# Field-pair tower on one core: single-tile transposes in the first part, gathers paced anew, finer signals at the end

## The chip, the cores and the metric

The kernel runs on 1 core of one Trainium2 chip. The metric is the device time of one execution in microseconds. The kernel before was timed three times: 1156.47, 1158.18 and 1160.94 us, with a median of 1158.18 us. The profile comes from another execution of the same kernel, which took 1160.57 us; its recorded span is 1158.8 us.

## The reference, cut to what matters

2048 samples have 40 ids each. Each id picks a row of 64 floats from its own table. For each of the 780 pairs of fields (i, j) there is a 64x64 matrix W, and the pair's value is `(e_i W) . e_j`. The 780 values and 16 dense numbers go through two layers with bias and ReLU (512 and 256 wide) and a last product to one number.

```python
e = jnp.stack([tbl_0[ids[:, 0]], ..., tbl_39[ids[:, 39]]], axis=1)   # 2048 x 40 x 64
viW = jnp.einsum('bpd,pde->bpe', e[:, i_idx, :], W)                  # 780 pairs
z = jnp.einsum('bpe,bpe->bp', viW, e[:, j_idx, :])
h = jnp.concatenate([z, dense_ctx], axis=1)
h = jnp.maximum(h @ W_top1 + b_top1, 0.0)
h = jnp.maximum(h @ W_top2 + b_top2, 0.0)
y = h @ W_top3
```

Everything is float32.

## The kernel before, in words

**Chunks, tiles, steps.** The samples are worked on in 4 chunks of 512. Two fields make a tile, so there are tiles 0 to 19. A chunk is 196 numbered steps; a step multiplies embeddings with weights on TensorE into one of three PSUM buffers `u`, and VectorE multiplies the result with the other embedding (`multiply`, L952 and L921). "Column" steps (L1038) then go through a second small matmul that sums (L1052). "Row" steps (L1024), 72 a chunk, are summed by ScalarE (L838, 16 pieces each), or by one VectorE reduction (L962), or by six GpSimd additions (L755), as lists fix in advance. Steps are counted through the kernel: chunk 1 begins at step 196, chunk 2 at 392, chunk 3 at 588. A step is over for the others when VectorE has made its product; the semaphore `prod_ready` counts that.

**The two parts of chunk 0.** Only chunk 0 is cut in two parts of 256 samples (q = 0 and 1), steps 0 to 97 and 98 to 195, so that work can begin when half of the gathers are in. There a column step is two columns of 256 samples ("two" steps).

**Gathers.** GpSimd issues an indirect DMA for each field and 128 samples (L734): 4 for a tile in a part, 8 for a tile in a whole chunk, 640 in all. Tiles 0 to 3 land in `first_fields`, the others in a ring of 4 tiles, `gathered`, in which a gather waits until the tile four before it has been transposed. From the second part on each gather also waits until a given step is over (`issue_step`): its due time minus 14 steps, or a steady pace, whichever is earlier. The steady pace of the second part begins at step `FIRST_PART` with 2 steps a field; that of chunks 1, 2 and 3 is in `CHUNK_STEPS`. GpSimd's own row sums stand in the same queue.

**Transposes.** TensorE transposes the gathered tiles (L996) two at a time, and ScalarE copies the pair into `emb` (L799, and L797 for a swapped copy of tile 4). `make_transpose_steps` puts each pair at a step: in the first part 2 steps before its first use, later `LANDING` steps after its last gather was issued. Transposes are put out in their list's order, so that one due early waits behind the one ahead of it in the list.

**The layers on top** of chunk c run in the middle of chunk c+1, in four groups at the steps of `TOP_STEPS`: they stand with the first transposes that come at least `TOP_FIRST` steps after the chunk's start. A group of layer 1 is 12 matmuls of 128x512 (L1084) and two of half height (L1090); the one group of layer 2 is 8 (L1096); the last layer is 8 small ones (L1103). ScalarE copies out each group with bias and ReLU (`copy_top`, L853). Those of chunk 3 stand alone at the kernel's end.

**What sets the order.** `make_order` writes one list, `ORDER`; TensorE, VectorE and ScalarE each go through it and take their own entries. GpSimd goes through `POOL_ORDER`. Nothing is reordered when it runs, so an instruction that waits holds all behind it on its engine.

In the words below T4 is the transpose of tile 4, T(4,5) of both at once.

Of the kernel before, what the change touches and what calls it, by code (L numbers as in the profile page):

```python
# [49 lines left out]
EARLY = 9  # L50
EARLY_EVERY = 2
# [8 lines left out]
TOP_FIRST = 18  # L60
# [120 lines left out]
def make_first():  # L181
# [5 lines left out]
    for q in range(PARTS):  # L187
# [202 lines left out]

def make_needs():
# [53 lines left out]


TRANSPOSES = [(c, i, q) for c in range(CHUNKS) for q in parts(c) for i in range(TSTEPS)]
TURN_OF = {x: n for n, x in enumerate(TRANSPOSES)}


def make_transpose_steps():

    out = []
    for c, i, q in TRANSPOSES:
        need = c * N + NEEDS[c, q, i]
# [8 lines left out]
        out.append((at, c, i, q))  # L464
# [145 lines left out]
def pair_tower(nc, ids, tables, w_pairs, w_rows, dense, w1, b1, w2, b2, w3, y):  # L610
# [6 lines left out]
    with ctx:  # L617
# [55 lines left out]
        top_ready = sem("top_ready")  # L673
        top_copied = sem("top_copied")
# [28 lines left out]
        def _(pool):  # L703
# [6 lines left out]
            def gather(c, q, t, e, s):  # L710
# [3 lines left out]
                if first and t < FT:  # L714
# [3 lines left out]
                    if c >= 2:  # L718
                        pool.wait_ge(rows_transposed, TURN_OF[c - 2, t // 2, len(parts(c - 2)) - 1] + 1)
                elif first and RING_USE[c, q, t] >= GRING:  # L720

                    at, part, tile = RING_ORDER[RING_USE[c, q, t] - GRING]
                    pool.wait_ge(rows_transposed, TURN_OF[at, tile // 2, part] + 1)
# [41 lines left out]
        def _(act):  # L765
# [19 lines left out]
            def copy_emb(c, i, q, o):  # L785
                act.wait_ge(rows_transposed, TURN_OF[c, i, q] + 1)
# [4 lines left out]
                if i == HUB // 2:  # L791
# [3 lines left out]
                    for h in (0, 1):  # L795
                        to, of = slice((1 - h) * DIM, (2 - h) * DIM), slice(h * DIM, (h + 1) * DIM)
                        nc.scalar.activation(emb_swap[to, c % 2, at], u[of, BUFFER[o], HUB % 2, at], ACT.Copy)  # L797
                first = emb_at(c, 2 * i)
                nc.scalar.activation(emb[:, first:first + 2, at], u[:, BUFFER[o], :, at], ACT.Copy).then_inc(emb_ready, 1)  # L799
# [41 lines left out]
            def copy_top(c, group, o):  # L841
                layer, first = TOPS[group]
                acc = u[:, BUFFER[o], :, :]
                act.wait_ge(top_ready, c * TOP_GROUPS + group + 1)
# [352 lines left out]
```

## Time and profile before

| | |
|---|---|
| median of 3 runs | 1158.18 us (1156.47 to 1160.94) |
| the profiled execution | 1160.57 us, span 1158.8 us |
| TensorE matmul busy | 1105.2 us (95%) |
| VectorE busy | 947.9 us (82%) |
| ScalarE busy | 859.5 us (74%) |
| GpSimd busy | 744.8 us (64%) |
| DMA | 98.02 MB, mean 85 GB/s |

TensorE is busy almost throughout, but "busy" there includes waiting inside the pipeline of matmuls; VectorE is busy 9 tenths or more in most slices between 58 and 319 us and has its long rests where a group of the top layers fills TensorE. GpSimd's 0.95 us for a gather is followed by about 0.3 us between two, so it is fully taken at 76% busy. The rows further down are from the timeline (start in us, length in us, engine, line, operation, result<-inputs, count, and in brackets how long the engine stood idle before it and what ended that), from the list of waits, and from tables of stretches.

### The profile page before, as it was taken

Reading aid. Unit: us, or ns where it says so; the run is one execution under the profiler, and the core shown is the slowest. Engines: PE = TensorE matmul, PEld = TensorE weight load, DVE = VectorE, ACT = ScalarE, POOL = GpSimd, SP = SyncE. Lnnn points to the kernel's source line nnn. Section 1 sums busy time; section 2 is a strip of 40 time slices with the busy share of each in tenths; the row PEclk is TensorE's granted clock in tenths of the full one; section 3 lists DMA queues with packets and bytes.
Section 4 is the critical chain, followed back from the end, with each engine's and each line's share of the span. In section 5 each row is a group of like instructions: output and inputs, shape, how many; then the busy total and the mean of one; then the engine's idle time right before and its main releaser. Section 6 shows DMA issues by size and latency. Waiting matters only on the chain.

```text
span 1158.8 us, 52361 instructions
## 1 busy us (share of the span) xinstructions
PE 1105.2 (95%) x21232; PEld 506.7 (44%) x21232; DVE 947.9 (82%) x830; ACT 859.5 (74%) x6607; POOL 744.8 (64%) x898
## 2 busy tenths in 40 slices
PE   2699989999999999999999999999999999999998
PEld 1356757665643333333363333333354333333333
DVE  0699878999859689999976689999984968999960
ACT  0677857999958569999965457898982845799971
POOL 7776777777756555778777567788777756522310
PEclk9999999999999999999999999999999999999999
DMA  6344444444423332232322232222222323211000
GB/s 187 83 121 131 125 121 121 130 139 130 103 52 87 86 88 72 76 86 76 77 63 78 71 93 76 76 78 77 77 68 49 94 73 93 70 58 58 19 3 18
DMA packets 60594, 98.02 MB, mean 85 GB/s; under 512 B 17072, under 2 KB 17088, under 8 KB 60352
## 3 DMA queue, kind: packets, MB, share of 16 engines
q1 hardware_dynamic: 35568, 64.57, 18.1%
q0 software_dynamic: 20480, 21.01, 9.3%
q10 hardware_dynamic: 4304, 9.09, 2.4%
q8 instruction: 167, 2.74, 1.0%
q14 instruction: 75, 0.61, 0.2%
HBM read 94.60 MB, written 0.01 MB: 82 GB/s over the span
## 4 chain that ended last, share of the span: by engine, by line
PE 76%; ACT 9%; POOL 5%; issue 5%; DVE 4%; DMA 1%; DVEq 0%; POOLq 0%
PE u L1038 30%; PE u L1024 18%; PE zacc L1052 15%; ACT row_prod L838 8%; PE u L1084 7%; PE u L996 3%; POOL gathered L734 3%; DVE prod L952 2%; PE u L1096 2%; POOL first_fields L734 1%; DVE row_prod L921 1%; POOL row_prod_p L755 1%; DMA gathered<-tbl,index 1%; PE u L1090 1%; PE u L1070 0%
## 5 line engine op out<-in xcount | busy, mean ns | idle before, releaser
L838 ACT ACTIVATE row_prod<-row_prod 128x64 f32<-128x64 f32 x3248 | 776.5, 242 | 65.9 <-DVE row_prod L921 65.7
L952 DVE TENSOR_TENSOR prod<-u,emb 128x1024 f32<-128x1024 f32 x496 | 588.8, 1217 | 102.0 <-PE u L1038 100.4
L734 POOL DMA_INDIRECT gathered<-tbl,index x512 | 484.7, 947 | 221.9 <-issue 121.5
L838 ACT ACTIVATION_READ_ACCUMULATOR row_prod<-row_prod 128x1 f32 x3248 | 613.1, 189 | 0.0
L1038 PE MATMUL u<-emb,weights 64*32 64x512 f32 (+1 forms) x9760 | 523.1, 507 | 3.5 <-DVE prod L952 2.1
L1024 PE MATMUL u<-row_weights,emb 64*32 64x512 f32 (+5 forms) x5632 | 337.7, 522 | 7.1 <-ACT emb L799 2.3
L1038 PEld LDWEIGHTS u<-emb,weights 64*32 64x32 f32 x9760 | 200.9, 107 | 235.7 <-issue 114.4
L921 DVE TENSOR_TENSOR row_prod<-u,first_fields 128x1024 f32<-128x1024 f32 x203 | 246.9, 1216 | 62.1 <-PE u L1024 61.8
L1052 PE MATMUL zacc<-prod,band 64*32 64x512 f32 (+1 forms) x4960 | 277.1, 504 | 0.7 <-DVE prod L952 0.5
L755 POOL TENSOR_TENSOR row_prod_p<-row_prod_p 128x512 f32<-128x512 f32 (+4 forms) x210 | 128.8, 614 | 90.8 <-DVE row_prod_p L921 77.1
L1024 PEld LDWEIGHTS u<-row_weights,emb 64*32 64x32 f32 x5632 | 118.4, 109 | 147.4 <-issue 56.7
L1052 PEld LDWEIGHTS zacc<-prod,band 64*32 64x32 f32 x4960 | 106.4, 107 | 115.4 <-issue 104.0
L734 POOL DMA_INDIRECT first_fields<-tbl,index x128 | 121.4, 948 | 49.9 <-issue 26.5
L799 ACT ACTIVATE emb<-u 128x1024 f32<-128x1024 f32 (+1 forms) x50 | 42.4, 849 | 86.5 <-PE u L996 86.3
L1084 PE MATMUL u<-z,w12s 128*128 128x512 f32 x192 | 85.6, 603 | 0.0
L853 ACT ACTIVATE h<-u,b1s 128x512 f32<-128x512 f32 x16 | 10.1, 684 | 80.6 <-PE u L1090 80.6
L1084 PEld LDWEIGHTS u<-z,w12s 128*128 128x128 f32 x192 | 36.4, 193 | 44.1 <-issue 43.7
L921 DVE TENSOR_TENSOR row_prod_p<-u,first_fields 128x1024 f32<-128x1024 f32 x42 | 51.1, 1217 | 4.5 <-PE u L1024 4.4
L921 DVE TENSOR_TENSOR row_prod_v<-u,first_fields 128x1024 f32<-128x1024 f32 x43 | 52.3, 1217 | 2.8 <-PE u L1024 2.6
L962 DVE TENSOR_REDUCE row_sums<-row_prod_v 128x16 f32<-128x1024 f32 x43 | 51.0, 1209 | 0.0
L996 PE MATMUL u<-ident,gathered 128*128 128x128 f32 x256 | 38.4, 284 | 13.2 <-DMA gathered<-tbl,index 12.8
L996 PEld LDWEIGHTS u<-ident,gathered 128*128 128x128 f32 x256 | 27.4, 142 | 40.7 <-DMA gathered<-tbl,index 14.4
(29 smaller groups left out, 151.9 us busy)
## 6 DMA issues: line engine op xcount, KB each, us to landing
weights<-w_pairs SPq DMA_DIRECT2D x155, 256.0 KB
row_weights<-w_rows SPq DMA_DIRECT2D x90, 256.0 KB
gathered<-tbl,index POOLq DMA_INDIRECT x512
w12s<-w_top ACTq DMA_DIRECT2D x8, 832.0 KB
first_fields<-tbl,index POOLq DMA_INDIRECT x128
w12s<-w_top ACTq DMA_DIRECT2D x4, 512.0 KB
index<-ids SPq DMA_DIRECT2D x1, 280.0 KB, 11.8
row_sums<-dense ACTq DMA_DIRECT2D x4, 32.0 KB
```

The lines of the kernel that those rows point to most:

```text
L734: pool.indirect_dma_start(out=to, out_offset=None, in_=tables[2 * t + e], in_offset=bass.IndirectOffsetOnAxis(ap=index[:, col:col + 1].bit ...
L755: nc.gpsimd.tensor_tensor(to, x[:, :, 0:width], x[:, :, width:2 * width], ALU.add).then_inc(rows_reduced_p if last else halved, 1)
L799: nc.scalar.activation(emb[:, first:first + 2, at], u[:, BUFFER[o], :, at], ACT.Copy).then_inc(emb_ready, 1)
L838: last = nc.scalar.activation(x, x, ACT.Copy, accum_out=row_sums[:, c % 2, s, q:q + 1])
L921: nc.vector.tensor_tensor(result, products, x, ALU.mult).then_inc(prod_ready, 1)
L952: nc.vector.tensor_tensor(result, products, x, ALU.mult).then_inc(prod_ready, 1)
L962: nc.vector.tensor_reduce(row_sums[:, c % 2, s, q:q + 2 * FF], x, mybir.AxisListType.X, ALU.add).then_inc(rows_reduced_v, 1)
L996: last = nc.tensor.transpose(u[:, b, h, s * P:(s + 1) * P], x, ident[:, :])
L1024: last = nc.tensor.matmul(u[g * TILE:(g + 1) * TILE, b, h, places], emb[half, emb_at(c, at // 2), samples_of], row_weights[half, x % PIECE ...
L1038: last = nc.tensor.matmul(u[of, b, h, to], weights[half, x % WRING, unit, of], y, start=True, stop=True)
L1052: last = nc.tensor.matmul(zacc[TILE * cg:TILE * cg + TILE, bank, samples(c, q)], band[half, TILE - 1 - r:2 * TILE - 1 - r], prod[half, (c ...
L1084: nc.tensor.matmul(u[:, b, m, :], w12s[:, x % 2, m * FULL + q, :], z_blocks(c, q)[:, 0, :], start=(q == 0), stop=False)
```

## The change

Five edits. In the first part of chunk 0 tiles 4 to 9 are transposed and copied one at a time, and `make_first` mixes the steps by single tiles, so that a row step of tile 4 may stand ahead of T5. `FIRST_PART` goes from 40 to 44 and `LANDING` of chunk 0 from 9 to 11, which puts the gathers of the second part 4 steps and its transposes 6 steps later. The pace of chunks 2 and 3 begins 3 steps earlier, and their transposes go with it, apart from T(10,11) of chunk 3 (step 609 in both). `TOP_FIRST` goes from 18 to 20; with the new steps that moves chunk 1's four top groups from steps 413, 433, 453, 473 to 430, 450, 470, 489; those of chunk 2 go from 609, 633, 653, 673 to 609, 630, 650, 670. And at the top ScalarE signals each copy by itself, a new semaphore `top_half` tells of the first half of a group, the half-height matmuls of layer 1's second group stand first in it, and layer 2's eight stand so that the first four need only layer 1's first two copies.

```diff
+SINGLE = range(4, 10)
-TOP_FIRST = 18
+TOP_FIRST = 20
-LANDING = (9, 17, 18, 18)
-FIRST_PART = 40
+LANDING = (11, 17, 18, 18)
+FIRST_PART = 44
-CHUNK_STEPS = {1: (115, 3.9), 2: (280, 4.9), 3: (480, 4.9)}
+CHUNK_STEPS = {1: (115, 3.9), 2: (277, 4.9), 3: (477, 4.9)}
...
-            for i in range(EARLY // 2 + 1):
-                now = [x for x in rows if max(tiles_used(x)) // 2 <= i]
-                ready = [x for x in twos if max(tiles_used(x)) // 2 <= i]
+            for t in [*range(1, SINGLE[0], 2), *SINGLE]:
+                now = [x for x in rows if max(tiles_used(x)) <= t]
+                ready = [x for x in twos if max(tiles_used(x)) <= t]
...
+def tiles_at(c, t, q):
+    return range(t, t + (1 if (c, q) == (0, 0) and t in SINGLE else 2))
...
-            def copy_emb(c, i, q, o):
-                act.wait_ge(rows_transposed, TURN_OF[c, i, q] + 1)
+            def copy_emb(c, t, q, o):
+                act.wait_ge(rows_transposed, TURN_OF[c, t, q] + 1)
...
-                first = emb_at(c, 2 * i)
-                nc.scalar.activation(emb[:, first:first + 2, at], u[:, BUFFER[o], :, at], ACT.Copy).then_inc(emb_ready, 1)
+                first, count = emb_at(c, t), len(tiles_at(c, t, q))
+                nc.scalar.activation(emb[:, first:first + count, at], u[:, BUFFER[o], 0:count, at], ACT.Copy
+                                     ).then_inc(emb_ready, 1)
...
                     for m in (0, 1):
+                        if m == 0 and group:
+                            act.wait_ge(top_half, c * (TOP_GROUPS - 2) + group)
+                        else:
+                            act.wait_ge(top_ready, c * TOP_GROUPS + group + 1)
                         to, bias = (h1, b1s) if layer == 1 else (h2, b2s)
-                        ins = nc.scalar.activation(to[:, first + m, :], acc[:, m, :], ACT.Relu,
-                                                   bias=bias[:, first + m:first + m + 1])
+                        nc.scalar.activation(to[:, first + m, :], acc[:, m, :], ACT.Relu,
+                                             bias=bias[:, first + m:first + m + 1]).then_inc(top_copied, 1)
...
-                    pe.wait_ge(top_copied, c * TOP_GROUPS + group)
-                    for m, q in itertools.product((0, 1), range(M1)):
+                    for m, q in ((0, 0), (1, 0), (0, 1), (1, 1), (1, 2), (0, 2), (0, 3), (1, 3)):
+                        if (m, q) == (0, 0):
+                            pe.wait_ge(top_copied, c * TOP_COPIES + LAYER1_COPIES[1])
+                        elif (m, q) == (1, 2):
+                            pe.wait_ge(top_copied, c * TOP_COPIES + LAYER1_COPIES[2])
+                        elif (m, q) == (0, 3):
+                            pe.wait_ge(top_copied, c * TOP_COPIES + LAYER1_COPIES[3])
...
-                    for q, g in itertools.product(range(M2), range(SUB)):
-                        last = nc.tensor.matmul(u[g * TILE:(g + 1) * TILE, b, 0, 0:P], w3s[:, q, :],
+                    for q in range(M2):
+                        pe.wait_ge(top_copied, c * TOP_COPIES + M1 + q + 1)
+                        for g in range(SUB):
+                            last = nc.tensor.matmul(u[g * TILE:(g + 1) * TILE, b, 0, 0:P], w3s[:, q, :],
```

TensorE's queue at the start, before: the transposes (`ident`) and the row steps of tiles 0, 4 and 5 to 7 (`row_weights`) behind steps 0 and 1.

```order
L996 MATMUL u<-ident,gathered 128x128 x4
...
L1024 MATMUL u<-row_weights,emb 32x128 x4
L1024 MATMUL u<-row_weights,emb 32x512 x16
L996 MATMUL u<-ident,gathered 128x128 x4
L1024 MATMUL u<-row_weights,emb 32x512 x24
L1038 MATMUL u<-emb,weights 32x256 x16
```

The same place now.

```order
L1025 MATMUL u<-ident,gathered 128x128 x2
...
L1053 MATMUL u<-row_weights,emb 32x128 x4
L1025 MATMUL u<-ident,gathered 128x128 x2
L1053 MATMUL u<-row_weights,emb 32x512 x16
L1025 MATMUL u<-ident,gathered 128x128 x2
L1053 MATMUL u<-row_weights,emb 32x512 x16
L1025 MATMUL u<-ident,gathered 128x128 x2
L1053 MATMUL u<-row_weights,emb 32x512 x16
L1067 MATMUL u<-emb,weights 32x256 x16
```

Before, T(4,5) stands ahead of steps 2 to 5 and T(6,7) ahead of steps 6 and 7. Now T4, T5, T6 and T7 stand apart, with two row steps (16 matmuls of 512) between them.

TensorE's queue at step 75, where the first transposes of the second part come, before.

```order
L1052 MATMUL zacc<-prod,band 32x256 x16
L996 MATMUL u<-ident,gathered 128x128 x4
L996 MATMUL u<-ident,first_fields 128x128 x8
L996 MATMUL u<-ident,gathered 128x128 x4
L1038 MATMUL u<-emb,weights 32x256 x16
L1024 MATMUL u<-row_weights,emb 32x512 x8
L1052 MATMUL zacc<-prod,band 32x256 x16
L1038 MATMUL u<-emb,weights 32x256 x48
L1052 MATMUL zacc<-prod,band 32x256 x16
L996 MATMUL u<-ident,gathered 128x128 x4
```

The same place now.

```order
L1081 MATMUL zacc<-prod,band 32x256 x16
L1025 MATMUL u<-ident,gathered 128x128 x4
L1025 MATMUL u<-ident,first_fields 128x128 x8
L1067 MATMUL u<-emb,weights 32x256 x16
L1053 MATMUL u<-row_weights,emb 32x512 x8
L1081 MATMUL zacc<-prod,band 32x256 x16
L1067 MATMUL u<-emb,weights 32x256 x16
L1025 MATMUL u<-ident,gathered 128x128 x4
L1067 MATMUL u<-emb,weights 32x256 x32
```

Four pairs stood together at step 75 (tiles 18 and 19 of the first part, tiles 0 to 5 of the second) and T(6,7) of the second part five steps behind. Now three stand together, T(4,5) comes at step 78 and T(6,7) at step 86.

TensorE's last queue entries, with the semaphores that they wait for, before.

```order
L1084 MATMUL u<-z,w12s 128x512 [waits w12_loaded0,z_copied]
L1084 MATMUL u<-z,w12s 128x512 x11
L1090 MATMUL u<-z,w12s 128x512 x2
L1096 MATMUL u<-h,w12s 128x512 [waits top_copied,w12_loaded1,z_copied]
L1096 MATMUL u<-h,w12s 128x512 x7
L1103 MATMUL u<-z,w3s 32x128 [waits top_copied,small_loaded]
L1103 MATMUL u<-z,w3s 32x128 x7
```

The same place now.

```order
L1111 MATMUL u<-z,w12s 128x512 [waits w12_loaded0,z_copied]
L1111 MATMUL u<-z,w12s 128x512
L1123 MATMUL u<-z,w12s 128x512 x12
L1140 MATMUL u<-h,w12s 128x512 [waits top_copied,w12_loaded1,z_copied]
L1140 MATMUL u<-h,w12s 128x512 x3
L1140 MATMUL u<-h,w12s 128x512 [waits top_copied]
L1140 MATMUL u<-h,w12s 128x512
L1140 MATMUL u<-h,w12s 128x512 [waits top_copied]
L1140 MATMUL u<-h,w12s 128x512
L1150 MATMUL u<-z,w3s 32x128 [waits top_copied,small_loaded]
L1150 MATMUL u<-z,w3s 32x128 x3
L1150 MATMUL u<-z,w3s 32x128 [waits top_copied]
```

The half-height pair has moved to the front of its group, and one wait for all copies has become several waits for one copy each.

## Rows read from the trace of the kernel before

**Rows 1.** Waits of TensorE: us in total, times, longest.
```profile
PE u L996 <- DMA first_fields<-tbl,index: 22.3, 4, 12.8
PE u L996 <- DMA gathered<-tbl,index: 12.8, 6, 3.4
```

**Rows 2.** Timeline of TensorE, steps 0 to 8: start, length, engine, operation, count, idle before.
```profile
25.80 5.07 PE L1024 MATMUL u<-row_weights,emb 64*32 64x256 f32 x112 [0.78 <-ACT emb L799]
...
34.86 5.84 PE L1024 MATMUL u<-row_weights,emb 64*32 64x320 f32 x112
...
44.27 0.44 PE L996 MATMUL u<-ident,gathered 128*128 128x128 f32 x2 [3.21 <-DMA gathered<-tbl,index]
44.63 4.50 PE L1024 MATMUL u<-row_weights,emb 64*32 64x512 f32 x48
```

**Rows 3.** Timeline of GpSimd: tile 7's last gather, three ring waits, chunk 1's tile 11.
```profile
41.84 0.95 POOL L734 DMA_INDIRECT gathered<-tbl,index  x1 [0.30 <-issue]
...
83.60 0.95 POOL L734 DMA_INDIRECT gathered<-tbl,index  x1 [0.79 <-PE u L996]
96.50 0.94 POOL L734 DMA_INDIRECT gathered<-tbl,index  x1 [3.20 <-PE u L996]
...
137.99 0.95 POOL L734 DMA_INDIRECT gathered<-tbl,index  x1 [1.76 <-PE u L996]
...
326.94 0.95 POOL L734 DMA_INDIRECT gathered<-tbl,index  x1 [0.31 <-DVE prod L952]
```

**Rows 4.** Timeline of VectorE: steps 8, 15, 75, 80, 83.
```profile
50.18 1.22 DVE L921 TENSOR_TENSOR row_prod<-u,first_fields 128x1024 f32<-128x1024 f32 x1
...
61.70 1.21 DVE L921 TENSOR_TENSOR row_prod<-u,first_fields 128x1024 f32<-128x1024 f32 x1
...
140.62 1.23 DVE L952 TENSOR_TENSOR prod<-u,emb 128x1024 f32<-128x1024 f32 x1 [2.47 <-PE u L1038]
...
150.82 1.23 DVE L921 TENSOR_TENSOR row_prod<-u,first_fields 128x1024 f32<-128x1024 f32 x1 [3.06 <-PE u L1024]
...
156.14 1.23 DVE L952 TENSOR_TENSOR prod<-u,emb 128x1024 f32<-128x1024 f32 x1 [0.53 <-PE u L1038]
```

**Rows 5.** ScalarE's groups by shape, 0 to 300 us: busy us, mean ns, idle before.
```profile
L799 ACT ACTIVATE emb<-u 128x512 f32<-128x512 f32 x20 | 11.8, 594 | 46.2 <-PE u L996 46.1
...
L797 ACT ACTIVATE emb_swap<-u 64x256 f32<-64x256 f32 x4 | 1.5, 379 | 9.4 <-PE u L996 9.3
```

**Rows 6.** Timeline of TensorE: T7 of the second part; T(10,11) of chunk 1.
```profile
149.26 0.44 PE L996 MATMUL u<-ident,gathered 128*128 128x128 f32 x2 [3.37 <-DMA gathered<-tbl,index]
...
336.51 1.09 PE L996 MATMUL u<-ident,gathered 128*128 128x128 f32 x8
```

**Rows 7.** Table of stretches: busy us and count per engine, granted clock, DMA.
```profile
152.00:154.00 2.00, 2.00 (x48) 1.24 (x40) 1.27 (x2) 1.92 (x16) 1.65 (x2) 0.50 0.67 161
```

**Rows 8.** Timeline of GpSimd: a row sum, and the first gather of chunk 3.
```profile
706.91 3.39 POOL L755 TENSOR_TENSOR row_prod_p<-row_prod_p 128x512 f32<-128x512 f32 x5
...
721.81 0.95 POOL L734 DMA_INDIRECT first_fields<-tbl,index  x1 [1.02 <-DVE prod L952]
```

**Rows 9.** Timeline of TensorE: T11 of chunk 3, top groups of chunks 2 and 3.
```profile
883.13 0.66 PE L996 MATMUL u<-ident,gathered 128*128 128x128 f32 x4 [2.32 <-DMA gathered<-tbl,index]
883.62 12.16 PE L1084 MATMUL u<-z,w12s 128*128 128x512 f32 x24
...
1134.10 10.57 PE L1084 MATMUL u<-z,w12s 128*128 128x512 f32 x24
```

**Rows 10.** The chain that ended last, in order of time: start, us, what.
```profile
1145.77 1.27 ACT h L853 x2
...
1147.18 7.12 PE u L1096 x16
...
1154.32 1.27 ACT z L853 x2
...
1155.73 0.68 PE u L1103 x16
```

More of the change, by code:

```diff
@@ L388 @@
 W12_BLOCKS = 2 * FULL + 1
+TOP_COPIES = M1 + M2 + 1
+LAYER1_COPIES = range(1, M1 + 1)
 def make_needs():
@@ L443, in issue_step, with make_transposes @@
     return max(1, int(min(in_time, steady)))
-TRANSPOSES = [(c, i, q) for c in range(CHUNKS) for q in parts(c) for i in range(TSTEPS)]
-TURN_OF = {x: n for n, x in enumerate(TRANSPOSES)}
+def tiles_at(c, t, q):
+    return range(t, t + (1 if (c, q) == (0, 0) and t in SINGLE else 2))
+def make_transposes():
+    out = []
+    for c in range(CHUNKS):
+        for q in parts(c):
+            t = 0
+            while t < T:
+                out.append((c, t, q))
+                t += len(tiles_at(c, t, q))
+    return out
+TRANSPOSES = make_transposes()
+TURN_OF = {(c, x, q): n for n, (c, t, q) in enumerate(TRANSPOSES) for x in tiles_at(c, t, q)}
 def make_transpose_steps():
     out = []
-    for c, i, q in TRANSPOSES:
-        need = c * N + NEEDS[c, q, i]
+    for c, t, q in TRANSPOSES:
+        i = t // 2
+        need = c * N + min(n for n, s in enumerate(STEPS[c]) if part_of(c, n) == q and {*tiles_at(c, t, q)} & {*tiles_used(s)})
         if c == 0 and q == 0:
@@ L463, in make_transpose_steps @@
             assert issued <= at <= need
-        out.append((at, c, i, q))
+        out.append((at, c, t, q))
     return out
@@ L673, in pair_tower @@
         top_ready = sem("top_ready")
+        top_half = sem("top_half")
         top_copied = sem("top_copied")
@@ L718, in gather @@
                     if c >= 2:
[L719 removed]
+                        pool.wait_ge(rows_transposed, TURN_OF[c - 2, t, len(parts(c - 2)) - 1] + 1)
                 elif first and RING_USE[c, q, t] >= GRING:
                     at, part, tile = RING_ORDER[RING_USE[c, q, t] - GRING]
[L723 removed]
+                    pool.wait_ge(rows_transposed, TURN_OF[at, tile, part] + 1)
                 if issue_step(c, q, 2 * t + e, s):
@@ L983, in buffer_free, with transpose_step @@
                 else:
-                    pe.wait_ge(top_copied, last[1] * TOP_GROUPS + last[2] + 1)
-            def transpose_step(c, i, q, b):
-                for h in (0, 1):
-                    t = 2 * i + h
+                    pe.wait_ge(top_copied, last[1] * TOP_COPIES + min(2 * last[2] + 2, TOP_COPIES))
+            def transpose_step(c, first, q, b):
+                for h, t in enumerate(tiles_at(c, first, q)):
                     if t < FT:
@@ L1014, in pair_step @@
                 t = max(tiles_used(step))
-                if (c, q, "tile", t // 2) not in seen:
-                    seen.add((c, q, "tile", t // 2))
-                    pe.wait_ge(emb_ready, TURN_OF[c, t // 2, q] + 1)
+                if (c, q, "tile", t) not in seen:
+                    seen.add((c, q, "tile", t))
+                    pe.wait_ge(emb_ready, TURN_OF[c, t, q] + 1)
                 if step[0] == "row":
@@ L1078, in top_group, with remainder @@
                 if layer == 1:
+                    def remainder(start):
+                        for m in (0, 1):
+                            half = slice(m * DIM, (m + 1) * DIM)
+                            last = nc.tensor.matmul(u[:, b, m, :], w12s[half, x % 2, 2 * FULL, :], z_blocks(c, FULL)[half, 0, :],
+                                                    start=start, stop=not start)
+                        return last
+                    if first:
+                        remainder(True)
                     for m in (0, 1):
@@ L1083, in top_group @@
                                                             (c, q // 2, len(parts(c)) - 1)])
-                            nc.tensor.matmul(u[:, b, m, :], w12s[:, x % 2, m * FULL + q, :], z_blocks(c, q)[:, 0, :],
-                                             start=(q == 0), stop=False)
+                            last = nc.tensor.matmul(u[:, b, m, :], w12s[:, x % 2, m * FULL + q, :], z_blocks(c, q)[:, 0, :],
+                                                    start=(first == 0 and q == 0), stop=(first > 0 and q == FULL - 1))
@@ L1086, in top_group @@
+                        if first and m == 0:
+                            last.then_inc(top_half, 1)
                     if first == 0:
                         pe.wait_ge(z_copied, Z_COPY[c, ROW_BLOCK + 2, 0])
-                    for m in (0, 1):
-                        half = slice(m * DIM, (m + 1) * DIM)
-                        last = nc.tensor.matmul(u[:, b, m, :], w12s[half, x % 2, 2 * FULL, :], z_blocks(c, FULL)[half, 0, :],
-                                                start=False, stop=True)
+                        last = remainder(False)
```

19 lines of the change are left out of this document (10 added, 9 removed).

## The prediction

> **What bounds the kernel now.** I read the waits of TensorE first: its named waits are mostly for gathers, 22.3 us for tiles 0 to 3 and 12.8 us for later tiles in six waits [rows 1]. The first sum is not touched by the change. Then I read the start in the timelines. GpSimd issues a gather every 1.25 us (0.95 us and 0.30 us between), so a tile of the first part needs 5.0 us of issue; tile 7's last one ends at 42.79 and its transpose starts at 44.27, 1.5 us later [rows 2, 3]. TensorE stood idle 3.21 us for it, with steps 6 and 7 queued behind although they need only tile 5. VectorE catches up from step 8 on: between its start at 50.18 and step 15 at 61.70 stand ten operations, 1.15 us apart, with no idle time beyond 0.1 us between two [rows 4]. From there into the 130s it is VectorE that sets the pace, so what is gained before step 8 is kept until something else comes last.
>
> Two later places stand out. At 149.26 the transpose of tile 7 of the second part waits 3.37 us for its gather, and after it the granted clock is 0.50 (1.2 GHz) for a while [rows 6, 7]. At 883.13 T11 of chunk 3 waits 2.32 us, and the 24 matmul records of the top group behind it take 12.16 us where the same group takes 10.57 us at the kernel's end, at full clock [rows 9]. At the end TensorE waits twice for two ScalarE copies of 1.27 us together [rows 10].
>
> **Term A, the start.** Before, steps 2 to 5 stand behind T(4,5), which waits for tile 5, and end at 40.70 (34.86 + 5.84) [rows 2]. Now T4 needs tile 4 alone, whose last gather ends 15.0 us before tile 7's, at 27.8, so that it lands at 29.3, before step 1 ends at 30.87. T4 takes about 0.4 us (44.27 to 44.63 for the two matmuls of T7), so steps 2 and 3 start at 31.3; T5 (landed 34.3) and steps 4 and 5 follow and end at 37.5 at the latest if the steps keep their 5.84 us. Tile 6 lands at 39.3. T6 and steps 6 and 7 need 0.4 us and at most 2 x 1.5 us (44.63 + 4.50 is three such steps at the slower rate [rows 2]), so TensorE is through at 42.7, before tile 7 lands at 44.3. T7 ends at 44.7, step 8 takes 0.9 to 1.5 us, and VectorE starts step 8 at 45.6 to 46.2 instead of 50.18: the same ten operations follow, since the five reductions on VectorE keep their places among them. That is 4.0 to 4.6 us; I take 4.4. Tiles 8 and 9 land 5 and 10 us after tile 7, at 49.3 and 54.3, before VectorE's queue asks for them (steps 15 and 19); T(10,11) at step 21 then meets tile 11, landing at 64.3, at about 63, which costs TensorE up to 1.4 us, within its buffers' lead.
>
> ScalarE gets six copies of 128x256 for three of 128x512. A copy of 512 takes 594 ns, one of 256 elements 379 ns on 64 partitions [rows 5]; so two cost 0.16 us more than one, 0.5 us in all. Between two copies it sums rows and has gaps: 46.2 us of its idle time stands ahead of such copies [rows 5]. I cost them at 0, bounds 0 and 0.5 us. The Trainium skill, "Perfetto Trace Analysis", Optimizing Scalar/DVE Operations, speaks against this edit: each ScalarE instruction carries a fixed access cost (some 50 ns of busy time on PSUM), so larger ones are better where the engine is saturated. By its figure the three extra copies would cost an estimated 0.15 us, by the rows 0.5 us; the page also says that breaking up helps where the engine isn't saturated but makes others wait, which is the case here.
>
> **Term B, the seam between the parts.** Before, four pairs of transposes stand together at step 75 and VectorE idles 2.47 us; T(6,7) at step 80 waits 3.37 us and then half clock follows, and VectorE's idle time from step 75 to step 83 adds to 7.34 us (2.47, 0.17, 3.06, 0.43, 0.68, 0.53) [rows 4]. Now T(6,7) stands at step 86. Without waits step 86 comes some 6 x 1.15 = 7 us behind step 80, and the wait was 3.4 us: it is gone if the lead of 4.4 us is matched by GpSimd. It is: GpSimd's stream is without idle time apart from three waits for the ring, 0.79, 3.20 and 1.76 us, less the usual 0.30 each: 4.85 us [rows 3]. These wait for T(12,13), T(14,15) and T(18,19), which all come as much earlier as the steps do. What stays is three pairs together (2.47 x 3/4 = 1.9 us) and two single ones at 0.5 us each (0.53 in rows 4 as the nearest). Gain 7.3 - 2.9 = 4.4 us; bounds 2 and 5.
>
> The pace of 44 and the transposes 6 steps later (which free the ring later) could hold GpSimd: of the second part tile 16's first gather now needs step 107 over and T(12,13) at step 110, tile 18's needs step 115 over and T(14,15) at step 118. With steps 8.8 us earlier than before and gathers 4.4 us earlier these fall within about 1 us of each other. I take no delay, bound 2 us.
>
> **Does the lead of 8.8 us survive chunk 1?** GpSimd issues without a break until tile 11 of chunk 1, whose last gather ends at 327.89 and lands at 329.4; its transpose stands at 336.51, 7.1 us later [rows 3, 6]. TensorE gains 8.8 us, GpSimd 4.4: 2.7 us of room are left. From tile 12 on gathers wait for steps and move along.
>
> **Term C, chunk 3.** GpSimd's stream is again full from the first gather of chunk 3 at 721.81, which waited for step 479 to end [rows 8], to tile 11. It now needs only step 476, about 3.4 us earlier, but a row sum of 3.6 us (3.39 and a last 0.22) for step 475 stands ahead of it now: it starts at about 719.0. Behind it, up to tile 11, stand 96 gathers as before and 10 row sums instead of 11. Tile 11 lands 2.8 + 3.6 = 6.4 us earlier in relation to the steps, T(10,11) stays at step 609, and the wait of 2.32 us goes with the slow stretch behind it (12.16 - 10.57 = 1.6 us): 3.9 us. The other transposes of chunks 2 and 3 come 3 steps earlier like their gathers. Chunk 1's top groups move 17 steps later; their own work is the same, I cost the move at 0, bounds -2 and +2 us, the size of one wait with its slow stretch.
>
> **Term D, the end.** Layer 2's first four matmuls need only copies that were made 10 us before, so the gap between 1145.77 and 1147.18 goes, 1.4 us. Its copies: h2's first half is copied beside the last matmul, so only one of two remains: 0.6 us. Half of the sixteen records of L1103 (0.68 us [rows 10]) run beside the second copy: 0.3 us. Together 2.3 us, bounds 1.4 and 2.7. The same edits in chunks 0 to 2 are hidden: TensorE has steps behind each group.
>
> **Sum.** 4.4 + 4.4 + 3.9 + 2.3 = 15.0 us. Against the profiled execution: 1160.57 - 15.0 = 1145.6. That execution is 2.4 us above the median of 1158.18, so the median after is 1143.2; I say 1143. By the bounds: the most is 4.6 + 5 + 4 + 2.7 + 2 = 18 us (1140), the least 4.0 + 2 + 3.9 + 1.4 - 2 - 0.5 = 9 us (1149).
>
> **The rivals.**
> 1. *The lead is given back to the gathers in chunk 1 (15%).* For it: the room of 2.7 us is small, and the later pace and ring waits can hold GpSimd in the second part. If GpSimd gains nothing, TensorE can be ahead by 7.1 us at 336.51, not 8.8, and the wait may bring one more slow stretch of 1.6 us: 1143 + 1.7 + 1.6 = 1146. If it comes 3 us later than before, 1149. Against it: each of the three ring waits shrinks with the steps.
> 2. *The start brings no lead (8%).* Idle time moves: TensorE now idles from 37.5 to 39.3 and before T7, and the clock may be at 1.2 GHz then. If steps up to 8 go at the slow rate and VectorE starts step 8 no earlier, term A is 0: 1147. The Trainium skill, "TensorE: Matmul & The Clock Gate", What's actually happening, says that the slow clock is the default and activity lifts it, so that rests between short bursts are what it punishes; of the half clock behind a rest rows 7 show an instance. Against it: tile 7's landing, not TensorE's rate, sets step 8.
> 3. *Chunk 3's wait stays (9%).* The top groups of chunk 1, now nearer to chunk 3's gathers, hold back GpSimd, and tile 11 is late as before: term C is 0, 1147.
> 4. *Slower than before (4%).* The same mechanism, larger: gathers wait while a top group fills TensorE, about 10 us for a layer-1 group (10.57 in rows 9). If two groups more fall into the issue of chunk 2's last tiles, chunk 3's stream starts some 17 us late. Its transposes at steps 532 to 609 have about 7 to 8 us of room (as the 7.1 us in chunk 1), so TensorE waits 9 us and after each of five waits a slow stretch follows, 8 us: 17 us lost against 11 won without term C, and 1164. It decides from about 12 us of delay on. Against it: groups at 430 to 489 are all but one over before the stream's first gathers are due at step 477.
> 5. *Only the end is faster (4%).* The edits of the first part cancel each other, 1155 to 1158.
>
> **Chances and range.** The forecast has 60%. Measurement tells about 0.5%, 5.8 us, from no change. Faster by more than that (below 1152.4) are the forecast, rivals 1 to 3: 0.90 with small losses to the neighbours; same 0.06, slower 0.04. The range of 8 in 10 holds the forecast with its bounds and rivals 1 to 3: 1137 to 1152.
>
> **What would show it.** In the profile after: steps 2 to 7 ahead of T7, VectorE's step 8 near 46; no wait of TensorE near 145 and no stretch at half clock there; T(10,11) of chunk 1 without a wait near 328; no wait for a gather at step 609 and 10.5 us for the group behind it; layer 2 right behind layer 1 at the end. Wrong would be a wait for gathers between 225 and 330, a step 8 later than 48, or the last 35 us shorter by less than 1.4 us.

## The result, and the profile after

The changed kernel takes 1145.96 us (median of 5, 1144.97 to 1146.48) beside 1158.12 us before (median of 5, 1156.15 to 1160.94): ratio 0.9893, 95% interval 0.988 to 0.9906. The forecast was 1143, range 1137 to 1152. The profiled execution took 1146.02 us (span 1144.2), against 1160.57 (span 1158.8) for the one before: 14.6 us less where the sum said 15.0.

The waits of TensorE after (us in total, times, longest), which answer to [rows 1]:

```profile
PE u L1025 <- DMA first_fields<-tbl,index: 22.1, 4, 13.1
PE u L1025 <- DMA gathered<-tbl,index: 3.0, 1, 3.0
PE u L1053 <- ACT emb L824: 3.0, 3, 1.3
PE u L1053 <- ACT z L843: 2.1, 1, 2.1
...
PE u L1150 <- ACT z L883: 0.3, 1, 0.3
```

Of six waits for later tiles (12.8 us) one of 3.0 us is left. The first tiles' 22 us are the same, as nothing touches them.

TensorE's timeline at the start after, for [rows 2] (start, length, engine, line, count, idle before):

```profile
31.27 4.17 PE L1053 MATMUL u<-row_weights,emb 64*32 64x320 f32 x80
35.37 0.44 PE L1025 MATMUL u<-ident,gathered 128*128 128x128 f32 x2
35.74 2.13 PE L1053 MATMUL u<-row_weights,emb 64*32 64x512 f32 x32
40.91 0.41 PE L1025 MATMUL u<-ident,gathered 128*128 128x128 f32 x2 [3.04 <-DMA gathered<-tbl,index]
41.25 3.63 PE L1053 MATMUL u<-row_weights,emb 64*32 64x512 f32 x32
44.81 0.44 PE L1025 MATMUL u<-ident,gathered 128*128 128x128 f32 x2
```

The wait now stands at T6, and the two steps behind it take 3.63 us where the two behind T5 take 2.13: it is followed by half clock (granted clock 0.50 from 41.4 to 44.6).

VectorE after, for [rows 4]: the products of steps 6, 8 and 15, then steps 75, 80 and 86 at the seam.

```profile
43.29 1.22 DVE L951 TENSOR_TENSOR row_prod<-u,first_fields 128x1024 f32<-128x1024 f32 x1 [2.68 <-PE u L1053]
...
46.89 1.22 DVE L951 TENSOR_TENSOR row_prod<-u,first_fields 128x1024 f32<-128x1024 f32 x1
...
58.78 1.23 DVE L951 TENSOR_TENSOR row_prod<-u,first_fields 128x1024 f32<-128x1024 f32 x1 [0.24 <-PE u L1053]
...
136.91 1.22 DVE L982 TENSOR_TENSOR prod<-u,emb 128x1024 f32<-128x1024 f32 x1 [1.84 <-PE u L1067]
...
144.52 1.21 DVE L951 TENSOR_TENSOR row_prod<-u,first_fields 128x1024 f32<-128x1024 f32 x1
...
151.73 1.22 DVE L982 TENSOR_TENSOR prod<-u,emb 128x1024 f32<-128x1024 f32 x1 [0.34 <-PE u L1067]
```

Against before that is 3.3 us earlier at step 8, 2.9 at step 15, 3.7 at step 75, 6.3 at step 80 and 7.8 at step 86, which starts at 159.5 before. I compared the start of the same step's product in both traces further on as well:

| step | before | after | difference |
|---|---|---|---|
| 8 | 50.2 | 46.9 | -3.3 |
| 75 | 140.6 | 136.9 | -3.7 |
| 86 | 159.5 | 151.7 | -7.8 |
| 140 | 231.2 | 224.0 | -7.2 |
| 300 | 468.0 | 461.0 | -7.0 |
| 355 | 533.0 | 527.8 | -5.3 |
| 588 | 850.8 | 842.9 | -7.9 |
| 609 | 898.1 | 886.0 | -12.0 |
| 783 | 1119.0 | 1107.2 | -11.8 |
| end of span | 1158.8 | 1144.2 | -14.6 |

So the time went in four places: the start, the seam, step 609 and the end. Later places in TensorE's timeline after, for [rows 6] and [rows 9]: T(6,7) of the second part, T(10,11) of chunk 1, a new wait near step 354, and T(10,11) of chunk 3 with the top group behind it.

```profile
149.94 0.66 PE L1025 MATMUL u<-ident,gathered 128*128 128x128 f32 x4
...
329.34 1.09 PE L1025 MATMUL u<-ident,gathered 128*128 128x128 f32 x8
...
525.44 1.09 PE L1053 MATMUL u<-row_weights,emb 64*32 64x512 f32 x16 [1.25 <-ACT emb L824]
...
872.45 1.09 PE L1025 MATMUL u<-ident,gathered 128*128 128x128 f32 x8
873.38 10.46 PE L1123 MATMUL u<-z,w12s 128*128 128x512 f32 x24
```

The waits of 3.37 and 2.32 us are gone, and the group of 24 takes 10.46 us instead of 12.16. There is no half clock behind T(6,7) either; the table of stretches has, for 150 to 152 us (us; busy us and count of PE, PEld, DVE, ACT, POOL; granted clock; DMA share; GB/s):

```profile
150.00:152.00 2.00, 2.00 (x53) 1.14 (x60) 1.66 (x3) 1.37 (x9) 1.60 (x2) 1.00 0.16 39
```

GpSimd's gather for tile 11 of chunk 1 stands here:

```profile
323.30 0.94 POOL L758 DMA_INDIRECT gathered<-tbl,index  x1 [0.30 <-issue]
```

It ends 3.6 us earlier than before (324.24 for 327.89), lands at about 325.7 if 1.5 us pass as behind tile 7 in [rows 3], and is wanted at 329.34: 3.6 us of room, where 2.7 were forecast.

The chain that ended last, from the last group on, for [rows 10]:

```profile
1123.25 10.50 PE u L1123 x24
1133.75 6.88 PE u L1140 x16
1140.63 0.02 issue
1140.65 0.69 ACT z L883
1141.35 0.04 issue
1141.39 0.47 PE u L1150 x8
1141.86 0.02 issue
1141.88 0.28 ACT h L887
```

Layer 2 follows layer 1 without a copy between them, one copy of 0.69 us stands where two took 1.27, and 8 records of layer 3 are left on the chain instead of 16. From the last product (step 783) to the end of the span it is 37.0 us for 39.8.

### The profile page after: what moved, and what is told of

Its sections match the earlier page's. It is cut to its first block, busy times and chain, and to the rows that moved or that the text cites. A ratio compares the mean times of both kernels' runs of the same rounds, so it can differ in the third digit from the quotient of the medians.

```text
span 1144.2 us, 52390 instructions
## 1 busy us (share of the span) xinstructions
PE 1103.2 (96%) x21232; PEld 507.6 (44%) x21232; DVE 947.9 (83%) x830; ACT 860.4 (75%) x6610; POOL 742.7 (65%) x898
## 4 chain that ended last, share of the span: by engine, by line
PE 81%; ACT 8%; DVE 4%; issue 3%; POOL 2%; DMA 1%; DVEq 0%
PE u L1067 32%; PE u L1053 19%; PE zacc L1081 16%; ACT row_prod L864 7%; PE u L1123 7%; PE u L1025 3%; DVE prod L982 3%; PE u L1140 2%; POOL first_fields L758 1%; DVE row_prod L951 1%; POOL gathered L758 1%; PE u L1111 1%; DVE row_sums L992 1%; PE u L1099 0%; ACT emb L824 0%
## 5 line engine op out<-in xcount | busy, mean ns | idle before, releaser
L1067 PEld LDWEIGHTS u<-emb,weights 64*32 64x32 f32 x9760 | 203.2, 107 | 233.9 <-issue 111.0
L824 ACT ACTIVATE emb<-u 128x1024 f32<-128x1024 f32 (+2 forms) x53 | 42.8, 810 | 85.5 <-PE u L1025 81.8
L1025 PEld LDWEIGHTS u<-ident,gathered 128*128 128x128 f32 x256 | 27.3, 141 | 31.9 <-issue 12.8
## 6 DMA issues: line engine op xcount, KB each, us to landing
index<-ids SPq DMA_DIRECT2D x1, 280.0 KB, 11.8
```

The costliest lines, as they stand in the source:

```text
L824: nc.scalar.activation(emb[:, first:first + count, at], u[:, BUFFER[o], 0:count, at], ACT.Copy).then_inc(emb_ready, 1)
L1025: last = nc.tensor.transpose(u[:, b, h, s * P:(s + 1) * P], x, ident[:, :])
L1067: last = nc.tensor.matmul(u[of, b, h, to], weights[half, x % WRING, unit, of], y, start=True, stop=True)
```

## The experiments

The theory was that the gain is the sum of four independent parts: the end (2.3 us), the single tiles (4.4), the pace with the seam (4.4) and chunk 3 (3.9). Its rivals were that the single tiles and the pace only work together, that chunk 3's wait goes by itself once the front is earlier, and that the end's edits are hidden. All kernels are the changed one with some of its edits undone. The one with the end alone is this:

```diff
-SINGLE = range(4, 10)
+SINGLE = ()
-TOP_FIRST = 20
+TOP_FIRST = 18
-LANDING = (11, 17, 18, 18)
+LANDING = (9, 17, 18, 18)
-FIRST_PART = 44
+FIRST_PART = 40
-CHUNK_STEPS = {1: (115, 3.9), 2: (277, 4.9), 3: (477, 4.9)}
+CHUNK_STEPS = {1: (115, 3.9), 2: (280, 4.9), 3: (480, 4.9)}
...
-            for t in [*range(1, SINGLE[0], 2), *SINGLE]:
+            for t in range(1, 10, 2):
```

**Four parts, first series.** The end alone, as above:

> Only the end's edits (copies signalled one by one, the half-height matmuls first, layer 2 reordered); steps, gathers and transposes as before. Theory: it acts at the kernel's end alone, since in chunks 0 to 2 TensorE has steps behind every group. The trace of the changed kernel ends 37.0 us after the start of the last VectorE product, that of before 39.8 us: 2.8 us, so 1158.1 - 2.8 = 1155.3 us. The waits of 3.4 us near 149 us and 2.3 us near 883 us stay. Rival: the finer signals also free ScalarE or PSUM buffers in the middle; then it is faster by over 4 us, below 1154.

The end and single tiles (`SINGLE` and its loop as in the changed kernel):

> The end's edits and the single transposes of tiles 4 to 9 with their step order; FIRST_PART, LANDING, CHUNK_STEPS and TOP_FIRST as before. Theory: the lead of the start (2.9 us from step 15 to step 60 in the changed kernel's trace) is carried through, since GpSimd's three ring waits shrink with it; the wait for tile 7 of the second part near 149 us and its half clock stay: 1155.3 - 2.9 = 1152.4 us. Rival: the lead is lost at the seam, where TensorE only waits longer for the gathers (4 to 6 us instead of 3.4): 1155.

The end and the pace (`FIRST_PART = 44`, `LANDING = (11, ...)`):

> The end's edits and FIRST_PART 44 with LANDING 11; pairs of transposes at the start and the old step order. Theory: the transpose of tiles 6 and 7 of the second part at step 86 no longer waits, and the slow stretch behind it goes; the changed kernel's lead grew from 3.0 to 8.3 us there and kept 7.2 us from step 140 on, so 4.3 us are kept: 1155.3 - 4.3 = 1151 us. Rival: this needs the start's lead too, because without it GpSimd is held by the pace of 44 (tile 16 waits for step 107 instead of 103), runs late into chunk 1, and TensorE waits for gathers between 225 and 330 us: 1154 or slower.

The end, single tiles and the pace:

> The end's edits, the single transposes and FIRST_PART 44 with LANDING 11; CHUNK_STEPS and TOP_FIRST as before. Theory: the gains add, 2.8 + 7.2 = 10.0 us by the traces, 1148.1 us, and the wait near 883 us (now near 876) stays. What is missing to the changed kernel's 1146.0 is then the worth of the edits to chunks 2 and 3, about 4 us by the traces' lead at step 610 (12.0 against 7.7 us), which would give 1150. Rival: the wait in chunk 3 is no longer there although its pace is unchanged, and the kernel stands at 1146.

These ran on a chip where the kernel before takes 1651.05 us instead of 1158. There they gave, as ratios to it: e1 0.9985 [0.9969, 1.0002], e2 0.9932 [0.9905, 0.9958], e3 0.9975 [0.9956, 0.9994], e4 0.9912 [0.9884, 0.9939]. None of the microseconds expected can be read off such a chip. Among these four the single tiles give most, and the pace adds nothing clear of the noise by itself (the intervals of e1 and e3 overlap). That this order holds at 1158 us is not shown; the traces there give the seam more than the start.

**Chunk 3 with the end** (`TOP_FIRST = 20`, `CHUNK_STEPS` 277 and 477):

> The end's edits, CHUNK_STEPS 277 and 477 and TOP_FIRST 20; the first part, FIRST_PART and LANDING as before. The four runs before this one ran at 1641 to 1651 us, the kernel before too (1651), with TensorE waiting for its own instructions; if this run is at 1158 us again for the kernel before, then: theory, the wait of 2.3 us for tile 11 of chunk 3 and the slow stretch behind it go, 4.3 us, and the end gives 2.8 us: 1158.1 - 7.1 = 1151 us, with the wait near 149 us still there. Rival: without the lead of the first chunk nothing changes for chunk 3's gathers relative to the steps, so the sum is the same; but if moving chunk 1's top groups by 17 steps costs something that the changed kernel's trace hides, it stands at 1153 or above.

0.9932 [0.9907, 0.9956], again on the 1651 us chip. There the gain beyond the end is some 9 us by the ratios, as much as that of the single tiles and twice what was expected; why, I didn't settle. That TensorE waits for its own instructions on this chip, as the expectation has it, no run shows: its profile has gaps with no wait named.

**The end alone, again.** The same kernel as e1:

> The kernel of e1 (only the end's edits) once more, to see whether the kernel before is at 1158 or at 1651 us this time. Theory: at 1158 it gives 2.8 us at the end and nothing elsewhere, 1155.3 us. If the kernel before is at 1651 us again, then about 2.4 us as in e1 (1648.7 against 1651.1), since the end's edits take away waits for ScalarE that TensorE's slower issue does not hide. Rival: the finer signals also help in the middle, over 4 us.

This ran on a chip of the first kind: 1156.83 us beside 1159.22, ratio 0.9976 [0.9965, 0.9987], so 2.8 us by the ratio and 2.4 by the medians. The end's edits are not hidden. TensorE's timeline of it, T7 of the second part and T11 of chunk 3:

```profile
151.13 0.69 PE L1025 MATMUL u<-ident,gathered 128*128 128x128 f32 x2 [3.11 <-DMA gathered<-tbl,index]
...
883.68 0.66 PE L1025 MATMUL u<-ident,gathered 128*128 128x128 f32 x4 [2.36 <-DMA gathered<-tbl,index]
884.18 12.16 PE L1123 MATMUL u<-z,w12s 128*128 128x512 f32 x24
```

Both waits and the slow group are there as in [rows 6] and [rows 9]: nothing is gained in front of the end, whose last product starts 0.6 us later than before (1119.63 and 1118.98).

**Second series of parts.** The same kernels as e2 to e5, the end with single tiles, with the pace, with both, and with chunk 3:

> The kernel of e2 (end's edits and the single transposes with their step order, all else as before), where the kernel before runs at about 1158 us. Theory: the lead of 2.9 us is carried through, because GpSimd's ring waits shrink with the steps; the wait near 149 us (now near 146) stays at about 3 us with its half clock. 1158.5 - 2.4 (measured for the end alone) - 2.9 = 1153 us. Rival: the lead is lost at the seam, the wait there grows to 5 or 6 us, and the kernel is at 1156.

> The kernel of e3 (end's edits and FIRST_PART 44 with LANDING 11), same setting. Theory: no wait for tile 7 of the second part and no half clock after it; the seam gives 5.3 us at step 86, of which about 1 us is given back by step 140: 1156.1 - 4.3 = 1152 us. Rival: without the start's lead the pace of 44 holds GpSimd back and TensorE waits for gathers in chunk 1 (225 to 330 us), with another stretch at half clock: 1155 or slower.

> The kernel of e4 (end, single transposes, FIRST_PART 44, LANDING 11; chunks 2 and 3 as before). Theory: the gains add: 1156.1 - 2.9 - 4.3 = 1149 us, and the wait for tile 11 of chunk 3 stays and makes up the remaining 3 to 4 us to the changed kernel. Rival: that wait is gone by itself and the kernel is within 1 us of 1146.

> The kernel of e5 (end's edits, CHUNK_STEPS 277 and 477, TOP_FIRST 20; first part as before). Theory: the wait near 883 us and the half clock behind it go, 4 us, nothing else: 1156.1 - 4 = 1152 us. Rival: the moved top groups and transposes of chunk 2 cost or give something of their own, over 1.5 us either way (in the changed kernel's trace the lead went from 7.0 us at step 300 to 5.3 at step 355 and to 7.5 at step 535).

They ran on another chip where the kernel before takes 1650.92 us, and repeat the first series within its intervals: 0.9942 [0.9918, 0.9965], 0.9972 [0.9954, 0.999], 0.9913 [0.9887, 0.9938] and 0.9941 [0.9919, 0.9964].

**The end, single tiles and pace, once more** (the kernel of e4 and e9):

> The kernel of e4 and e9 (end, single transposes, FIRST_PART 44 and LANDING 11; chunks 2 and 3 as before), once more, for a chip on which the kernel before runs at about 1158 us. Theory: the end is worth 2.4 us (measured), start and seam together 7.2 us by the traces' lead at step 300, the wait for tile 11 of chunk 3 stays: 1158.5 - 9.6 = 1149 us. Rival: the wait of chunk 3 is gone by itself, 1146; or start and seam are worth only what is left of 12.2 when 2.4 and 4.3 are taken off, 5.5 us, 1150.5. If the kernel before is at 1651 us again, 1637 as in e4 and e9.

1149.44 us beside 1159.43, ratio 0.9912 [0.9897, 0.9928]. From e6's 0.9976 that is 7.4 us for single tiles and pace together. The rest to the changed kernel's 0.9893 is 2.2 us for chunk 3 by the ratios, 3.5 us by the medians (1149.44 to 1145.96, on two occasions on which the kernel before differs by 1.3 us). The intervals of these two ratios overlap (0.9897 to 0.9928, 0.988 to 0.9906), so the worth of chunk 3's edits by themselves rests on the traces. Its timeline at T11 of chunk 3:

```profile
876.75 0.66 PE L1025 MATMUL u<-ident,gathered 128*128 128x128 f32 x4 [2.39 <-DMA gathered<-tbl,index]
877.24 10.47 PE L1123 MATMUL u<-z,w12s 128*128 128x512 f32 x24
```

That refutes the rival: the steps in front of it come 6.4 us earlier than before, and the wait is still 2.39 us. Chunk 3's stream of gathers begins when a step is over, so it came earlier with the steps (first gather at 715.66 instead of 721.81) and nothing was won against them. It takes the edits to `CHUNK_STEPS` and `TOP_FIRST` to remove the wait; which of the two does it, no run separates. But the group behind it takes 10.47 us, not 12.16. Its table of stretches (us; busy us and count of PE, PEld, DVE, ACT, POOL; granted clock; DMA share; GB/s):

```profile
880.00:884.00 4.00, 4.00 (x10) 1.72 (x10) 0.00 (x0) 0.00 (x0) 3.29 (x5) 1.00 0.13 25
```

The same place in the kernel before:

```profile
884.00:888.00 4.00, 4.00 (x7) 1.62 (x6) 0.00 (x0) 0.85 (x1) 2.96 (x4) 0.57 0.14 25
```

The clock stayed at 2.4 GHz (1.00) here, and was down for most of the stretch (0.57) there, after waits of the same length (2.39 and 2.32 us).

**A version beyond the change.** In the changed kernel TensorE waits 2.08 us at 314.01 for ScalarE's copy of z, since row sums of a later chunk stand in ScalarE's queue ahead of it. The edit holds them back past the turn:

```diff
-            if held or j < len(order) and steps < HOLD and order[j][0] != "turn":
+            if held or j < len(order) and steps < HOLD and (order[j][0] != "turn" or order[j][1] < o[1]):
...
-            out += held
-            held = []
+            out += [x for x in held if x[1] <= o[1]]
+            held = [x for x in held if x[1] > o[1]]
...
-        if o[0] in ("transpose", "top", "copy z") and (i + 1 == len(order) or order[i + 1][0] != "top"):
+        if (o[0] in ("transpose", "top", "copy z") or o[0] == "turn" and o[2]) and (i + 1 == len(order) or order[i + 1][0] != "top"):
```

> The changed kernel with one more edit: ScalarE's row sum of step 202 (which belongs to chunk 1) no longer stands ahead of the copy of chunk 0's first turned rows but behind that copy and the one of T(8,9); the sum of step 210 goes behind the second turned copy. The computation is the same. [...] The copy of the turned rows starts when it is ready, about 309 us, and not at 312.96 us, so the wait of 2.1 us at 314 us goes, and with it the half clock at 314.4 us (3.4 us long, 1.7 us of work lost): 3.8 us, 1146.0 - 3.8 = 1142 us (ratio to the kernel before 0.986). Rival: the wait goes, but TensorE and VectorE meet the next wait at once, since ScalarE is fully busy there and step 210 needs the ring place that the sum of step 202 frees later now: 1145 to 1146, ratio 0.989. If it is a chip on which the kernel before runs at 1651 us, nothing follows.

1144.26 us (median of 4, 1142.9 to 1145.97) beside 1157.87, ratio 0.9882 [0.9864, 0.99]. ScalarE's copy of z and VectorE's product of step 207 in it:

```profile
310.16 1.00 ACT L843 ACTIVATE z<-u 128x1024 f32<-128x1024 f32 x1
...
314.40 1.22 DVE L951 TENSOR_TENSOR row_prod<-u,first_fields 128x1024 f32<-128x1024 f32 x1 [0.16 <-PE u L1053]
```

The same two in the changed kernel, with TensorE's step between them:

```profile
312.96 1.00 ACT L843 ACTIVATE z<-u 128x1024 f32<-128x1024 f32 x1
...
314.01 1.67 PE L1053 MATMUL u<-row_weights,emb 64*32 64x320 f32 x28 [2.08 <-ACT z L843]
...
316.81 1.23 DVE L951 TENSOR_TENSOR row_prod<-u,first_fields 128x1024 f32<-128x1024 f32 x1 [3.39 <-PE u L1053]
```

The wait and the half clock after it are gone there. That execution was 0.8 us behind the changed kernel's at step 206, 3.0 us ahead at step 210 and 1.9 at step 217: 3.8 us won, 1.1 given back. More than half of what was given back is a wait for chunk 1's tile 11, for which the steps have now come too early:

```profile
327.90 0.66 PE L1025 MATMUL u<-ident,gathered 128*128 128x128 f32 x4 [0.68 <-DMA gathered<-tbl,index]
```

At the end of the span 2.0 us are left, where 3.8 were expected. In the runs the intervals of the two ratios overlap (0.9864 to 0.99, 0.988 to 0.9906), so a gain over the changed kernel is seen in the traces and not shown by the runs.

## Why the prediction was right, step by step

**Start: right in mechanism, one third too large.** Steps 2 to 7 do run ahead of T7, and step 8 came at 46.89 instead of 45.6 to 46.2: 3.3 us for 4.4. Two sizes were off. "Tile 6 lands at 39.3" rested on the one landing time of 1.5 us behind its gather; the last gather of tile 6 ended at 37.67 and T6 could start at 40.91, 3.2 us later (2.2 us later in e11, at 39.88, and 2.7 in e12, at 40.24). The trace before had both sizes: 1.5 us for tiles 5 and 7, and 3.4 us for tile 9, whose last gather ends at 52.80 and whose transpose, at 56.22, waits for it. And the prediction asked only what TensorE needs for step 8. VectorE does three operations, 3.6 us, between the product of step 6 (43.29) and that of step 8 (46.89), as it did before (46.59 and 50.18); so step 8 is 3.6 us behind step 6, and step 6 is tied to T6. What the edit does is to let VectorE follow tile 6 instead of tile 7: from 44.27 to 40.91, 3.4 us, not tile spacing's 5.0. The profiled e11 and e12 had step 8 at 46.13 and 45.93, inside the forecast, so the term is 3.3 to 4.2 us over three executions. The half clock in rival 2 did occur, at 41.3 and again at 55.0, and cost 1.5 us at T6 (3.63 - 2.13), but the kernel before had it behind T7 too (4.50 us for three steps in [rows 2]), so that one took little from the gain. The one at 55.0 it had not, and the lead fell from 3.3 us at step 8 to 2.9 at step 15. The Trainium skill, "TensorE: Matmul & The Clock Gate", What's actually happening, has the slow clock as the default that rests fall back to; this stretch agrees, and e11's 10.47 us at 877.24 is an instance where a rest of 2.39 us didn't bring it.

ScalarE's split copies were costed at 0: in the trace after six copies of 128x256 take 374 ns each and TensorE waits for none of them.

**Seam: 4.4 forecast, 4.5 measured at step 86** (-3.3 at step 8 to -7.8). T(6,7) of the second part at 149.94 waits for nothing and step 75's idle time is 1.84 us (forecast 1.9). Then some is given back: the pairs of transposes moved to steps 126 and 134 leave single gaps of VectorE of about half a us, and 7.2 us are left at step 140. The prediction had priced those transposes where they left and not where they went. Start and seam together are 7.2 us by this trace, for 8.8 forecast, and it is the best of three: in e11 the lead over before falls from 7.5 us at step 86 to 5.7 at step 140, in e12 from 7.5 to 5.9, and in both GpSimd waits 1.51 us for the ring at 196, where the prediction took no delay. That the runs of e6 and e11 give 7.4 us agrees with the 7.2 in part by luck: 1.7 us of e11's lead come only at step 609, where its group runs at full clock. How start and seam divide on this kind of chip rests on the traces alone; the runs that separate them were made on the slower chips, so that the single tiles and the pace work only together is not excluded at 1158 us.

**Chunk 1: right.** T(10,11) at 329.34 doesn't wait, and rival 1 fell: chunk 1's gathers start at 204.67 instead of 208.05, 3.4 us earlier, and tile 11's last one ends 3.6 us earlier, beside steps that come 7.2 us earlier; the difference of 3.5 us (7.17 - 3.65) fits into the room of 7.1 us. In e12 the steps are 9 us ahead and chunk 1's tile 11 only 2.1 us, and the wait of 0.68 us is there: here the room ends.

**Chunk 3: wait and slow group right, 4.1 us at step 609** (-7.9 at step 588, -12.0 at step 609; forecast 3.9). The last gather of tile 11 now ends 4.5 us ahead of T(10,11) (867.91 and 872.45); before, T11 started 1.5 us behind it, wait included. e11 shows that the wait needs these edits. It also shows that the 1.6 us of half clock is not a sure part of the term: with it the edit is worth 4 us, without it about the wait's 2.4; the runs, whose intervals overlap, say 2.2 to 3.5. "The move of chunk 1's top groups costs 0, bounds -2 and 2" held as well, though not because nothing happened: 1.7 us of the lead were lost between steps 300 and 355, a wait of 1.25 us for ScalarE's emb copy at 525.44 among it, and were back by step 520. The moved groups, which stand at steps 430 to 489, come too late to cause the loss. It goes with the edits to chunks 2 and 3: e12 has them, and has the wait (1.26 us at 523.60) and the loss; e11 and e6 have neither edit nor loss. These wait, like before, 1.5 us for another emb copy near step 518 (1.53 us at 766.35 before), for which the changed kernel waits 0.95 us (at 755.00).

**End: 2.3 forecast, 2.8 us by the trace, 2.4 to 2.8 us by the runs of e6.** All three pieces are in the chain; what is beyond them lies in the layers themselves, such as 6.88 us for layer 2 instead of 7.12.

**The base.** The sum of 15.0 against 14.6 is close in part by luck. Start and seam came 1.6 us short (7.2 for 8.8), and 0.5 us more at the end, 0.2 more in chunk 3 and some 0.7 won between steps 140 and 588 nearly made up for it; and chunk 3's term holds 1.7 us of half clock that need not have been there. By medians the change is worth 12.2 us, and the forecast is 3 us too low for that: before's profiled execution was 2.4 us above its median, and after's lies at its median (1146.02 and 1145.96). Subtracting 2.4 us from the result assumed that the same excess would go with both; part of what the change removes are just the waits with uncertain slow stretches, which may have made some executions longer. The 5 runs before spread over 4.8 us and those after over 1.5 us, which fits, and was not tested further.

**Rivals.** 1 (the lead is given back), 3 (chunk 3's wait stays) and 4 (slower) are excluded by the trace, 5 (only the end) by e6 and e11, and of 2 (no lead at the start) only the half clock came true.

## What to carry to other kernels

Where an edit lets a consumer start on an earlier tile, ask which engine the next step waits for after that: here VectorE's three operations behind step 6 took over from the tile's landing, and the gain was the difference of two landings and not the spacing of tiles. One landing time read from a trace is one of several sizes: 1.5 to 3.4 us here. Price a moved group of instructions at the place where it arrives too, and take the half clock behind a short wait as a likelihood and not as a sum. A stream that issues without a break is a second clock in such a kernel. If its first gather waits for a step, it moves along with what is won in front, and a wait for it stays as it is until the stream starts earlier against the steps (chunk 3 in e11); if it starts by itself, what is won in front uses up the room ahead of it (chunk 1 in e12).

## What the runs showed that was not expected

**Two kinds of chip.** On two of the chips the same kernel took 1651 us, not 1158. Engine busy time (share of the span, instructions) of the end-only kernel there:

```profile
PE 1467.7 (89%) x21232; PEld 655.7 (40%) x21232; DVE 961.2 (59%) x830; ACT 874.4 (53%) x6607; POOL 743.6 (45%) x898
```

And of the same kernel on a chip of the first kind (e6):

```profile
PE 1106.0 (96%) x21232; PEld 505.9 (44%) x21232; DVE 948.2 (82%) x830; ACT 860.4 (74%) x6607; POOL 742.7 (64%) x898
```

VectorE, ScalarE and GpSimd are busy as long as elsewhere, within 2%; TensorE's matmuls are drawn out. The waits of TensorE in the end-only kernel there begin with:

```profile
PE u L1053 <- issue: 47.4, 69, 2.4
PE u L1067 <- issue: 41.1, 75, 1.5
PE zacc L1081 <- issue: 26.1, 48, 1.5
```

115 us of idle time in 192 gaps in which no wait is seen. Once the gathers are over the steps run at full speed. The last gather of e7 is issued at 1475; a table row and the timeline of TensorE behind it:

```profile
1500.00:1520.00 20.00, 20.00 (x384) 7.10 (x376) 20.00 (x19) 20.00 (x169) 6.57 (x12) 1.00 0.20 56
...
1563.62 1.07 PE L1053 MATMUL u<-row_weights,emb 64*32 64x512 f32 x16
1564.48 1.07 PE L1081 MATMUL zacc<-prod,band 64*32 64x512 f32 x16
1565.34 1.07 PE L1067 MATMUL u<-emb,weights 64*32 64x512 f32 x16
```

Sixteen matmuls start every 0.86 us here, and steps 700 to 783 take 93.9 us on both kinds of chip, while steps 612 to 700 take 158 us against 123. The granted clock is 0.96 over the span, which doesn't explain it. Some 490 us over 640 gathers are 0.77 us a gather. From 1500 to 1520 us other DMA still moves 56 GB/s and GpSimd still adds (6.57 us), and the pace is full: 384 matmul records in 20 us, as in the kernel before behind its gathers. So neither of these is enough to draw the matmuls out; it is bound to the time of the gathers and to TensorE, and what makes it so is open.

**Half clock after a short wait comes and goes.** After waits of 2.32 and 2.36 us (before, e6) the group behind took 12.16 us, after 2.39 us (e11) 10.47; at 323 in e6 a wait of 2.12 us was followed by full clock (1.00), in the changed kernel at 314 one of 2.08 us by half (0.56 from 314 to 317). A wait of 1.82 us at 53.99 in the changed kernel was followed by half (0.50 from 55 to 57), one of 1.81 us at 53.05 in e12 was not. So the length of the wait alone doesn't decide it; which it will be I could not tell from what these traces show.
